# A deformable-convolution block on one core: the second conv's second half, nine steps in the third tap instead of three in the second and six in the third

## The reference

```python
out_normal = _conv(x, w_normal)
offset = jnp.concatenate([_conv(x, w_offx), _conv(x, w_offy)], axis=1)
out_x = _deform_conv(x, offset, w_dx)
out_y = _deform_conv(x, offset, w_dy)
out = _conv(jnp.concatenate([out_normal, out_x, out_y], axis=1), w_fusion)
out = jax.nn.relu(_bn(out, bn1_g, bn1_b, bn1_m, bn1_v))
out = _bn(_conv(out, w_conv2), bn2_g, bn2_b, bn2_m, bn2_v)
return jax.nn.relu(out + x)
```

## Time and profile before

| | |
|---|---|
| median of the runs | 2826.48 us |
| profiled execution, its own time | 2828.01 us |
| its span, first to last instruction | 2826.2 us |
| mean granted TensorE clock | 0.935 of full speed |
| PE, PE weight load, DVE, ACT, POOL busy | 86%, 84%, 79%, 71%, 73% of the span |
| moved by DMA | 522 MB, 185 GB/s |

### The profile page before, as it was taken

The page is one execution under the profiler, slowest core; times in us unless marked ns, Lnnn a source line. Parts: engine busy times, 40 slices in busy tenths (PEclk is TensorE's granted clock), DMA queues, the critical chain, the costliest instruction groups (busy, mean ns, idle before and its releaser), DMA issues. The chain is left out here.

```text
span 2826.2 us, 47580 instructions
## 1 busy us (share of the span) xinstructions
PE 2417.3 (86%) x15680; PEld 2365.9 (84%) x15680; DVE 2246.8 (79%) x5321; ACT 2017.9 (71%) x4817; POOL 2076.2 (73%) x1808
## 2 busy tenths in 40 slices
PE   3678888888888888888888888888888888888998
PEld 3578888888888888888888888888888888888898
DVE  5888878888778888888878888888888887788873
ACT  5777777777777777777777777777777777777751
POOL 6777777777777777777777777777777777777740
PEclk7889999999999999999999999999999999999999
DMA  5766666666666666666666666666666666666640
GB/s 182 221 184 193 193 191 190 190 189 190 191 190 191 196 193 192 186 190 189 191 188 190 190 192 191 189 187 187 186 189 190 190 187 188 191 191 205 182 121 29
DMA packets 162822, 522.45 MB, mean 185 GB/s; under 512 B 30992, under 2 KB 31120, under 8 KB 162576
## 3 DMA queue, kind: packets, MB, share of 16 engines
q0 software_dynamic: 144000, 471.97, 58.3%
q1 hardware_dynamic: 18576, 47.44, 4.8%
HBM read 506.18 MB, written 13.11 MB: 184 GB/s over the span
## 5 line engine op out<-in xcount | busy, mean ns | idle before, releaser
L309 POOL DMA_INDIRECT cells<-in_cells,index x1800 | 2064.0, 1147 | 647.3 <-issue 365.7
L467 ACT ACTIVATE samp<-cells,wgt 128x128 f32<-128x128 f32 x1800 | 662.3, 400 | 373.3 <-DVE cells L675 371.4
L467 ACT ACTIVATE cells<-cells,wgt 128x256 f32<-128x256 f32 x1800 | 775.7, 499 | 157.2 <-DMA cells<-in_cells,index 154.8
L675 DVE SCALAR_TENSOR_TENSOR cells<-cells,wgt 128x256 f32<-128x256 f32 x1800 | 746.4, 478 | 26.4 <-ACT cells L467 24.9
L682 DVE SCALAR_TENSOR_TENSOR samp<-cells,wgt,samp 128x128 f32<-128x128 f32 x1800 | 508.2, 345 | 19.1 <-ACT samp L467 18.6
L357 PE MATMUL acc<-samp_hi,w_hi 128*128 128x320 f32 x1440 | 476.2, 331 | 7.6 <-ACT feat L466 7.6
L360 PE MATMUL acc<-samp_lo,w_hi 128*128 128x320 f32 x1440 | 466.0, 324 | 0.0
L357 PE MATMUL work<-part_hi,w_hi 128*128 128x320 f32 x1440 | 464.4, 322 | 0.6 <-ACT off_s L466 0.6
L363 PE MATMUL acc<-samp_hi,w_lo 128*128 128x320 f32 x1440 | 462.9, 321 | 0.0
L363 PE MATMUL work<-part_hi,w_lo 128*128 128x320 f32 x1440 | 450.5, 313 | 0.0
L360 PE MATMUL work<-part_lo,w_hi 128*128 128x320 f32 x1440 | 450.1, 313 | 0.0
(11 more groups left out here) (87 smaller groups left out, 3831.2 us busy)
## 6 DMA issues: line engine op xcount, KB each, us to landing
cells<-in_cells,index POOLq DMA_INDIRECT x1800, 3.8
x_raw<-in_xflat SPq DMA_DIRECT2D x40, 410.0 KB, 4.3
late<-in_x SPq DMA_DIRECT2D x40, 320.0 KB, 5.4
out<-late SPq DMA_DIRECT2D x40, 320.0 KB, 3.3
late<-in_weights SPq DMA_DIRECT2D x5, 576.0 KB, 5.4
cells<-in_weights SPq DMA_DIRECT2D x1, 657.0 KB, 4.0
samp<-in_weights SPq DMA_DIRECT2D x1, 576.0 KB, 6.1
cst<-in_const SPq DMA_DIRECT2D x1, 199.0 KB, 4.7
```

The source lines that it names most:

```text
L309: eng.indirect_dma_start(out=cells[:, g, :], out_offset=None, in_=table[0:(b + 1) * CELLS, :], in_offset=bass.IndirectOffsetOnAxis(ap=inde ...
L467: return eng.activation(dst, src, ACT.Copy, scale=scale)
L675: eng.scalar_tensor_tensor(out=cells[:, g, 0:2 * C], in0=cells[:, g, 2 * C:4 * C], scalar=wgt[:, par, 1, 0, j, k:k + 1], in1=cells[:, g, 0 ...
```

## The change

C of part 1 is no longer split. The second tap's slice keeps the two halves of O; the third tap's slice has all nine steps of C of part 1. Nothing else is changed in the text. Since `conv` gives its pace marks at every third of its steps, the second tap's slice now gives none and its `deform_tap` all five; the third tap's slice gives three and its `deform_tap` two.

```diff
 SLICES = [
     [("C", 0, 0, 9)],
-    [("O", 0, 0, 3), ("O", 1, 0, 3), ("C", 1, 0, 3)],
-    [("C", 1, 3, 9)],
+    [("O", 0, 0, 3), ("O", 1, 0, 3)],
+    [("C", 1, 0, 9)],
     [("F", 0, 0, 9)],
```

## The result

The changed kernel takes 2716.14 us (median, 2715.54 to 2724.01) against 2826.47 us: a ratio of 0.9618, 95% interval 0.9600 to 0.9636. The profiled execution has a span of 2713.9 us.

What follows compares the result with a forecast made beforehand. GpSimd was taken as nearly full, delayed by PE's stall on off_c, and as setting the strip afterwards. 2826.2 - 86.6 (gather waits) + 1.4 (last strip) = 2741 us; range 2718 to 2780.

Steps and rivals of the forecast that it cites:

- The stall and its path: Second tap: PE's 5.62 us wait for off_c delays turned samples, samp_hi, samp_lo, next indices and GpSimd's gather; 2.83 us removable.
- The two waits that I put at 1.6 and 1.7 us: PE idle before turning tap 3's samples (1.6) and before C1's bank is free (1.7), replacing the 5.62 us wait.
- GpSimd sets the strip: After the change GpSimd's 45 gathers and their pauses, 65.6 us a strip, bind above the loop's 65.27.
- The waits taken off it: Removing all real waits before GpSimd's gathers in the 35 strips saves 86.6 us, 2383.4 to 2297.
- The gather's length: GpSimd's mean gather stays at 1154 ns in the 35 strips; 1119 ns was the alternative, from strips 1 to 3.
- the mechanism as a rival: VectorE's shifted two-SBUF-input groups catch more GpSimd gathers: two more a strip give 2878 us; slower had chance 0.03.
- its good end: Gathers shorten towards 1119 ns, so the loop binds instead of GpSimd: 2729 us; to 2733 had chance 0.16.
- The loop's 65.27 us: Strip length by the loop through turned samples, VectorE's samples and the gathers: 68.10 less the 2.83 us wait.
- my sum for the low side: If the loop binds instead of GpSimd: 2826.2 - 99 + 1.4 = 2729 us; to 2733 had chance 0.16.
- The clock: Rival: PE's idle times lower its clock, 0.6 us a strip, 2762 us; clock or longer gathers had chance 0.24.
- The idle time of 3.0 us: PE, ready early for the fifth tap, waits 3.0 us for samp_lo, possibly lowering its clock.
- The last strip: Without an offset conv, nine C1 matmuls move behind PE's idle time there: 1.4 us lost once, 2.4 at half clock.

Runs made afterwards that it cites:

- the longer lag: The kernel before the change with the pace lag at 7 taps instead of 5, C1 still split: 2825.12 us, 0.9983 of before.

## Why the prediction was right, and where its size was off

**The stall and its path: right, step by step.** The two waits that I put at 1.6 and 1.7 us are 1.79 and 1.34. The indices start 9.33 us after off_c (9.4 forecast), samp_hi and samp_lo run without their waits. The kernel with the samples turned late shows that the gain needs the path through `turned`: C1 whole, a shorter wait, and no gain. That the marks by themselves are worth next to nothing is shown by the longer lag (2825 us).

**GpSimd sets the strip: right for most strips.** Strips are its own time in the changed kernel (64.87 and 64.85 us), and one gather less makes them 0.84 us shorter. The waits taken off it were put at 86.6 us and are 85.4. But in 11 of the 35 strips the last tap's first gather waits for samples again, by 0.1 to 0.2 us: the next limit is reached there.

**The gather's length: the term that was mis-sized.** "I take 1154, as these strips have the same work" is the step that failed: 1136 ns, 27.5 us less in all. 85.4 + 27.5 is the 112.9 that the strips gained. The work was the same; its place against the gathers was not, and that sets their length, as the kernel with one SBUF input less shows. The two traces agree: gathers above 1.5 us that end behind `samp` go from 109 to 66, those behind the fusion's parts from 90 to 140, and those of 2.3 us and more from 73 to 63. How far the mean falls is luck in part: the four kernels with C1 whole, all gathers, and only ScalarE's order changed or nothing lie between 1120 and 1142 ns. I had the mechanism as a rival, with the wrong sign as its main case, and priced its good end only by strips 1 to 3.

**The loop's 65.27 us: too long.** I took 2.83 us off the old strip as if the rest of the loop kept its length. But 20 gathers lay in that loop: from the last tap's first, which waits for the samples of k = 5 (the prediction's "fifth tap"), to the third tap's last of the next strip. ScalarE stood 0.82 us for that one's cells, with x_hi for the next offset conv behind them:

```profile
1392.01 0.51 ACT L467 ACTIVATE cells<-cells,wgt 128x256 f32<-128x256 f32 x1 [0.82 <-DMA cells<-in_cells,index]
1392.42 0.42 ACT L466 ACTIVATE feat<-work 128x320 f32<-128x320 f32 x1
1392.74 0.88 ACT L466 ACTIVATE x_hi<-x_raw 128x820 fp32r<-128x820 f32 x1
```

These 20 took 25.3 us a strip on average, long ones among them, and take 24.0 in the changed kernel. There another loop binds the short strips. GpSimd's first gather of the last tap in two strips, and PE between them:

```profile
592.42 1.08 POOL L309 DMA_INDIRECT cells<-in_cells,index  x1 [0.45 <-DVE samp L682]
...
655.70 1.07 POOL L309 DMA_INDIRECT cells<-in_cells,index  x1 [0.45 <-DVE samp L682]
```

```profile
594.10:625.90 31.80, 31.80 (x221) 1.00 0.67 186
```

Both gathers wait 0.45 us for the samples, where a pause of 0.305 would stand, so the loop between them takes 63.28 us. Followed back from the second by releasers, it holds no gather: VectorE works from 626.84 on with no more than 0.91 us of idle time at once, the accumulators' copy before that waits for PE, and PE has no idle time back to 594.1, before which it waited for VectorE's step right behind the samples of 592.4. In one strip each, the same chain stands behind the 63.37 us with five gathers less and the 63.13 us with one SBUF input less. So the strips did not stop at 65.3, as my sum for the low side assumed. GpSimd alone, busy (count), clock, DMA share and GB/s of five strips:

```profile
626.10:689.40 63.30, 49.75 (x45) 1.00 0.69 202
...
754.00:820.40 66.40, 52.53 (x46) 0.97 0.66 196
...
1338.30:1403.80 65.50, 51.78 (x46) 0.95 0.67 197
1403.80:1469.50 65.70, 51.98 (x46) 1.00 0.67 198
...
1987.80:2051.10 63.30, 49.73 (x45) 0.95 0.68 202
```

The strips differ by 3.1 us and GpSimd's busy time by 2.8.

**The clock: it fell, and it was free.** In the strip from 1338.3 it fell after the two idle times, in the next it stayed up; stretches of both during C1 (columns of the earlier trace rows):

```profile
1353.50:1359.00 5.50, 4.97 (x19) 4.98 (x20) 5.37 (x14) 5.37 (x14) 4.28 (x5) 0.50 0.64 184
1419.60:1424.00 4.40, 4.39 (x30) 4.39 (x31) 4.40 (x12) 4.31 (x11) 3.25 (x4) 1.00 0.64 181
```

The strips are 65.5 and 65.7 us long, GpSimd's 51.8 and 52.0 us busy: C1 at 1.2 GHz cost nothing. Nor does it show in the short strips: those from 626.1 and from 1987.8 had a clock of 1.00 and 0.95 on average and both take 63.3 us. The idle time of 3.0 us that I feared at PE's fifth tap is 1.40 us (1435.12), for the larger part because I had overlooked a wait: with C1 early the fusion's first matmul, whose bank holds the turned offsets, waits 0.94 us for off_s.

**The last strip: right in kind.** ScalarE's accumulator copies at its end, before and then after:

```profile
2743.25 1.30 ACT L466 ACTIVATE feat<-acc 128x640 f32<-128x640 f32 x2 [1.26 <-PE acc L363]
```

```profile
2630.71 1.30 ACT L466 ACTIVATE feat<-acc 128x640 f32<-128x640 f32 x2 [1.25 <-PE acc L363]
```

It takes 58.51 instead of 57.15 us from the mark before, 1.36 us more; I put the nine matmuls behind the wait at 1.4. PE's idle time there has grown from 3.07 us to 4.34:

```profile
2584.39 1.30 PE L391 MATMUL turned<-cst,samp 128*128 128x128 f32 x5 [4.34 <-DVE samp_lo L633]
```

That the size agrees so well is partly luck: with the longer lag, where C1 is not regrouped, the last strip takes 57.79 us.

**The range** ended at 2718 because of the gather and the loop together: with both as measured, 2826.2 - 112.9 + 1.4 would have been 2715.

## What to carry to other kernels

Price a stall by what is queued behind it on its engine: here a matmul's wait for a bank cost nothing any more once the transposes that ScalarE needs stood ahead of it, and moving them back cost the whole gain though the wait stayed shorter. When an engine whose instructions contend with another's becomes the bound, do not carry its mean duration over to a new order, but give it the spread of its strips as a range on both sides. A loop's length measured on the old kernel contains the old durations of every engine in it, and once it is shorter, another loop may bind.

## What was not expected of the hardware

The gathers from GpSimd, most often 0.95 us, stretch to 3.0 us beside VectorE instructions with two SBUF inputs, and all above 1.5 us end 0.81 to 0.84 us after the end of such an instruction. In 126 of 222 cases it is the last of its run, in the others another with two SBUF inputs follows. Taking one of the two inputs from PSUM shortens the mean by 95 ns with VectorE's own times unchanged. The Trainium skill, "SBUF — State Buffer", section "Who interferes with whom", says that such VectorE instructions contend with GpSimd's reads of SBUF. The runs agree that they hold the gathers; that it is by a gather's reads, no run here shows. Not every gather that overlaps such a run is held, though: which ones are was not tried and stays open. Two kernels that differ only in ScalarE's order (2684 and 2720 us) can so lie 36 us apart, and in all kernels here in which GpSimd no longer waits the strip is 45 gathers and their pauses to within 0.1 us.
